# Token scores within halves of 64 rows: column halves of the array, a softmax over 64 columns, and mixing as two products with zero-padded weights

## The reference, cut to what matters

```python
xv = x.reshape(n, b, t, d).transpose(1, 0, 3, 2)        # t = 16, d = 192
q = jnp.einsum('bndt,st->bnds', xv, Wq) + bq            # s: 8
kv = jnp.einsum('bndt,st->bnds', xv, Wkv) + kv_bias     # k: 8, v: 8
q = q * scale
attn = jax.nn.softmax(jnp.einsum('bnds,bndr->bnsr', q, k), axis=-1)
out = q.transpose(0, 1, 3, 2) + jnp.einsum('bnsr,bndr->bnsd', attn, v)
```

## Time and profile before

| what | value |
|---|---|
| device time, median of 3 runs | 964.21 us (962.97 to 966.08) |
| the profiled execution: its own time | 967.46 us |
| its span, first to last instruction | 965.2 us, 25885 instructions |
| busy share: PE, PEld | 97%, 84% |
| busy share: DVE, ACT, POOL | 81%, 67%, 70% |
| mean granted TensorE clock | 0.988 |

### The profile page before, as it was taken

How to read it: one execution, slowest core, us unless ns; L and a number is a source line. 1 busy time by engine, 2 the same in 40 slices (tenths; PEclk the granted TensorE clock), 3 DMA queues, 4 the chain that set the end, 5 groups by cost and what they waited for, 6 DMA issues and landing times.

```text
span 965.2 us, 25885 instructions
## 1 busy us (share of the span) xinstructions
PE 934.8 (97%) x7402; PEld 814.2 (84%) x7402; DVE 781.2 (81%) x1996; ACT 645.7 (67%) x2501; POOL 673.6 (70%) x968
## 2 busy tenths in 40 slices
PE   5788999999999999999999999999999999999998
PEld 3667888889888889898888988888889888898877
DVE  3678888888888888888888888888888888888863
ACT  2456766676776676776667677667777666767763
POOL 2665777776677777677777767777767778776770
PEclk8899999999999999999999999999999999999999
DMA  6025444456444445544445554444554444555440
GB/s 199 24 70 143 129 121 126 127 149 160 134 130 120 129 128 160 156 121 126 129 121 149 160 138 131 117 128 129 159 158 121 130 125 123 145 160 146 110 118 17
DMA packets 193423, 124.68 MB, mean 129 GB/s; under 512 B 30720, under 2 KB 184960, under 8 KB 193408
## 3 DMA queue, kind: packets, MB, share of 16 engines
q1 hardware_dynamic: 190528, 121.05, 46.3%
q10 hardware_dynamic: 2880, 3.44, 1.1%
HBM read 69.39 MB, written 55.05 MB: 129 GB/s over the span
## 4 chain that ended last, share of the span: by engine, by line
PE 92%; DVE 3%; DMA 2%; issue 1%; POOL 1%; ACT 1%; SPq 1%; ACTq 0%; DVEq 0%; POOLq 0%
PE ring L1039 15%; PE bank L1058 13%; PE ring L1077 10%; PE bank L1251 7%; PE ring L1017 7%; PE ring L1251 7%; PE ring L1113 6%; PE ring L1157 4%; PE bank L1113 3%; PE ring L1163 3%; PE ring L1212 3%; PE ring L1182 3%; PE bank L1157 2%; PE bank L1233 2%; PE bank L1163 1%; PE bank L1203 1%
## 5 line engine op out<-in xcount | busy, mean ns | idle before, releaser
L335 ACT ACTIVATE E<-ring,m_neg 128x128 f32<-128x128 f32 x768 | 269.8, 383 | 9.9 <-DVE m_neg L684 8.9
L546 POOL TENSOR_TENSOR E<-E,e_rcp 128x512 f32<-128x512 f32 x158 | 175.6, 1111 | 91.5 <-DVE e_rcp L707 89.0
L538 POOL TENSOR_TENSOR qkT<-rot_c,rot_s 128x256 f32<-128x256 f32 x256 | 188.8, 738 | 20.1
L335 ACT ACTIVATION_READ_ACCUMULATOR E<-ring,m_neg 128x1 f32 x768 | 170.8, 222 | 0.0
L536 POOL TENSOR_TENSOR rot_s<-rot_s,rope_qs 128x256 f32<-128x256 f32 x192 | 140.8, 733 | 20.0 <-DVE rot_s L678 20.0
L1058 PE MATMUL bank<-wout_sb,G 128*128 128x192 f32 x744 | 152.0, 334 | 0.0
L684 DVE TENSOR_REDUCE m_neg<-ring 128x4 f32<-128x512 f32 x192 | 127.2, 676 | 11.2 <-PE ring L1077 11.2
L1058 PEld LDWEIGHTS bank<-wout_sb,G 128*128 128x128 f32 x744 | 118.7, 190 | 15.2 <-issue 11.5
L698 DVE STREAM_TRANSPOSE EB<-E 128x512 f32<-128x512 f32 x186 | 125.3, 689 | 1.5 <-POOL E L546 0.8
L1077 PE MATMUL ring<-qkT 64*128 64x128 f32 x1536 | 105.6, 285 | 0.4 <-POOL qkT L538 0.4
L1077 PEld LDWEIGHTS ring<-qkT 64*128 64x128 f32 x1536 | 93.2, 192 | 13.4 <-issue 9.1
(11 more groups left out here) (159 smaller groups left out, 2494.6 us busy)
## 6 DMA issues: line engine op xcount, KB each, us to landing
spill<-EB SPq DMA_DIRECT2D x186, 256.0 KB, 2.3
ET<-spill SPq DMA_DIRECT2D x248, 128.0 KB, 2.8
ET<-spill SPq DMA_DIRECT2D x248, 64.0 KB, 2.4
x_sb<-in_x_dram SPq DMA_DIRECT2D x64, 192.0 KB, 2.6
out_dram<-out_sb SPq DMA_DIRECT2D x31, 192.0 KB, 2.5
x_sb<-in_x_dram SPq DMA_DIRECT2D x64, 64.0 KB, 2.4
w_raw<-in_w_att_dram ACTq DMA_DIRECT2D x2, 608.0 KB, 5.8
win_raw<-in_w_in_dram ACTq DMA_DIRECT2D x2, 384.0 KB, 6.4
```

What stands on the lines that cost most here:

```text
L335: last = nc.scalar.activation(E[:, a, s * P:(s + 1) * P], RING[a][:, s * P:(s + 1) * P], ACT.Exp, bias=m_neg[:, a, s:s + 1], accum_out=e_s ...
L538: nc.gpsimd.tensor_tensor(qkT[:, b, :, a], rot_c[:, b, :, a], rot_s[:, b, :, a], ALU.add).then_inc(q_out, 1)
L546: nc.gpsimd.tensor_tensor(e, e, r, ALU.mult).then_inc(prob_out, 1)
```

## The change

Each query row only meets keys of its own half (rows 0 to 63 or 64 to 127), since blocks of 8 don't cross row 64. The changed kernel computes only the two 64x64 squares on the diagonal of each score matrix and keeps them beside each other: rows on 128 partitions, 64 columns per sequence. `tok_scores` issues eight calls of 64 output columns by 64 moving columns, with the lower and the upper column half of the array in turn, in place of four calls of 128 by 128. Mask, t_s, t_e, t_a, t_aT, t_c, t_d and bias_qv have 64 columns per sequence in place of 128. Because t_aT of both halves now shares its columns, `tok_mix` needs two products over 128 columns with weights bd_v[:, i] that are zero in the other half's rows, in place of one over 256. The layout of t_m turns from (a, i) to (i, a). At the start, bd_v takes two products of 64 partitions and two memsets on DVE.

```diff
-    blk = (row[:, None] // T2 == row[None, :] // T2)
+    blk = (row[:, None] % (P // 2) // T2 == row[None, 0:P // 2] // T2)
...
-        t_s, t_e, t_a, t_aT = (sb(n, [P, 2, P]) for n in ("t_s", "t_e", "t_a", "t_aT"))
+        t_s, t_e, t_a, t_aT = (sb(n, [P, 2, P // 2]) for n in ("t_s", "t_e", "t_a", "t_aT"))
...
-        t_c, t_d = sb("t_c", [P, 2, P]), sb("t_d", [P, 2, P])
+        t_c, t_d = sb("t_c", [P, 2, P // 2]), sb("t_d", [P, 2, P // 2])
...
-            nc.vector.tensor_tensor(bd_v[:].rearrange("p (b t) -> p b t", t=T), blk_keys[:].rearrange("p (b t) -> p b t", t=T),
-                                    wrep[:, 2 * T2:2 * T2 + T].rearrange("p (o t) -> p o t", o=1).broadcast_to([P, 8, T]),
-                                    ALU.mult).then_inc(s_bd, 1)
+            for i in range(2):
+                own = slice(i * (P // 2), (i + 1) * (P // 2))
+                nc.vector.tensor_tensor(bd_v[own, i].rearrange("p (b t) -> p b t", t=T),
+                                        blk_keys[own].rearrange("p (b t) -> p b t", t=T),
+                                        wrep[own, 2 * T2:2 * T2 + T].rearrange("p (o t) -> p o t", o=1).broadcast_to([P // 2, 8, T]),
+                                        ALU.mult).then_inc(s_bd, 1)
+                nc.vector.memset(bd_v[(1 - i) * (P // 2):(2 - i) * (P // 2), i], 0.0).then_inc(s_bd, 1)
...
-            nc.vector.transpose(t_aT[:].rearrange("p a (j c) -> p a j c", j=NB),
-                                t_a[:].rearrange("p a (j r) -> p a j r", j=NB)).then_inc(aT_out, 1)
+            nc.vector.transpose(t_aT[:].rearrange("p a (j c) -> p a j c", j=2),
+                                t_a[:].rearrange("p a (j r) -> p a j r", j=2)).then_inc(aT_out, 1)
...
                     for a in range(2):
-                        last = group(TOK_S[:, a * P:(a + 1) * P], (
-                            (qkT1[:, a, 0:P], qkT1[:, a, P:DP]), (qT2[:, a], kT2[:])))
+                        for k, (q, key) in enumerate(((qkT1[:, a, 0:P], qkT1[:, a, P:DP]), (qT2[:, a], kT2[:]))):
+                            for i in range(2):
+                                own = slice(i * (P // 2), (i + 1) * (P // 2))
+                                last = nc.tensor.matmul(TOK_S[own, a * (P // 2):(a + 1) * (P // 2)], q[:, own], key[:, own],
+                                                        start=(k == 0), stop=(k == 1))
                     last.then_inc(s_mm, 1)
...
-                    nc.tensor.matmul(TOK_M, bd_v[:], t_aT[:].rearrange("p a c -> p (a c)"),
-                                     start=True, stop=True).then_inc(m_mm, 1)
+                    for i in range(2):
+                        last = nc.tensor.matmul(TOK_M[:, i * P:(i + 1) * P], bd_v[:, i], t_aT[:].rearrange("p a c -> p (a c)"),
+                                                start=True, stop=True)
+                    last.then_inc(m_mm, 1)
```

More of the change, by code:

```diff
@@ L106, in program @@
         TOK_QK, TOK_REST = RING[1][:, 0:512], RING[1][:, 512:512 + DP]
[L107 removed]
+        TOK_S, TOK_M, TOK_H = RING[1][:, 512 + DP:512 + DP + P], B7[:, 0:DP], RING[0][:, 512:512 + 2 * D]
         HIDDEN = (RING[0][:, 1024:1536], B6[:], RING[1][:, 512:1024])
@@ L120, in program @@
         rope_kc, rope_ks, rope_qc, rope_qs = (sb(n, [P, P]) for n in ("rope_kc", "rope_ks", "rope_qc", "rope_qs"))
-        smask, blk = sb("smask", [P, P]), sb("blk", [P, P // 2])
+        smask, blk = sb("smask", [P, P // 2]), sb("blk", [P, P // 2])
         half_neg, warm = sb("half_neg", [P, 2]), sb("warm", [P, 2])
@@ L125, in program @@
         wrep, blk_keys = sb("wrep", [P, 2 * T2 + T]), sb("blk_keys", [P, P])
-        bd_qk, bd_v = sb("bd_qk", [P, P]), sb("bd_v", [P, P])
+        bd_qk, bd_v = sb("bd_qk", [P, P]), sb("bd_v", [P, 2, P])
         bqk_row, bias_rows = sb("bqk_row", [P, DP]), sb("bias_rows", [P, 1])
-        bias_sc, bias_qv, t_bias = sb("bias_sc", [P, 1]), sb("bias_qv", [P, P]), sb("t_bias", [P, 2])
+        bias_sc, bias_qv, t_bias = sb("bias_sc", [P, 1]), sb("bias_qv", [P, P // 2]), sb("t_bias", [P, 2])
         w_raw1, w_raw2 = sb("w_raw1", [P, NW]), sb("w_raw2", [P, NW])
@@ L552, in token_bias @@
                     need(pool, bias_sum, 2 * n)
-                    nc.gpsimd.tensor_tensor(t_c[:], t_a[:], bias_qv[:].rearrange("p (o c) -> p o c", o=1).broadcast_to([P, 2, P]),
+                    nc.gpsimd.tensor_tensor(t_c[:], t_a[:], bias_qv[:].rearrange("p (o c) -> p o c", o=1).broadcast_to([P, 2, P // 2]),
                                             ALU.mult).then_inc(bias_out, 1)
@@ L779, in tok_mixed @@
                     need(dve, h_mm, n)
-                    nc.vector.tensor_tensor(t_m[:].rearrange("p a i s -> p (a i) s"),
+                    nc.vector.tensor_tensor(t_m[:].rearrange("p i a s -> p (i a) s"),
                                             TOK_M.rearrange("p (x s) -> p x s", x=4),
@@ L801, in token_qk @@
                     if isinstance(p, int) and p == -1:
-                        dve.wait_ge(s_bd, 3)
+                        dve.wait_ge(s_bd, 6)
                     nc.vector.tensor_tensor(qkT1[:], TOK_QK.rearrange("p (a c) -> p a c", a=2),
@@ L1196, in tok_mix @@
                     if first == "tok":
-                        pe.wait_ge(s_bd, 3)
+                        pe.wait_ge(s_bd, 6)
                     if att and fin:
@@ L1211, in tok_h @@
                         for i in range(2):
-                            last = nc.tensor.matmul(TOK_H[i * (P // 2):(i + 1) * (P // 2), a * D:(a + 1) * D], t_m[:, a, i],
+                            last = nc.tensor.matmul(TOK_H[i * (P // 2):(i + 1) * (P // 2), a * D:(a + 1) * D], t_m[:, i, a],
                                                     x_sb[:, i, a], start=True, stop=True)
@@ L1374, in laid_out @@
         "bq_row": np.tile(tok_bq[None, :], (P, P // T2)),
-        "bv_row": np.tile(tok_bkv[None, :], (P, P // T2)),
+        "bv_row": np.tile(tok_bkv[None, :], (P, P // T2 // 2)),
         "w_att1": w_att[0:P], "w_att2": np.concatenate([w_att[P:D], w_att[P:D]], axis=0),
```

4 lines of the change are left out of this document (2 added, 2 removed).

## The result

The changed kernel takes 951.42 us (median of 6 runs, 950.03 to 952.64). The kernel before, run beside it, takes 964.38 (6 runs, 962.97 to 967.18). The ratio is 0.9843, with a 95% interval of 0.9827 to 0.9859. Against the 964.21 us of the prediction that is 949.1 us. The prediction said 953.9, from 950.5 to 960.5: right in the sign, too small in the size, and 1.4 us outside the range. The two medians alone stand 12.96 us apart, a ratio of 0.9866, just above that interval and inside the range (951.2 us); the record doesn't show where the difference between the two ratios comes from.

What follows compares the result with a forecast made beforehand. PE's own stream was taken to set the loop's time. Savings of 8.7 us (loop and pair 31), 0.3 (p = 1), 1.0 (p = 0) and 0.3 (p = -1) made 10.3: from median 964.21 to 953.9 us, range 950.5 to 960.5.

Steps and rivals of the forecast that it cites:

- a saving of 0.27 a step: tok_scores in each step: 0.885 us becomes 0.61, from a shape change, an exposed first load and 8 pairs at 0.058.
- (B): Rival: a pair stays at 0.111 us or the halves don't start together; about 967.5 us, slower; chance 0.09.
- (D): Rival: pairs near 0.09 us, so PE gains nothing and only some 2 us remain; 962.3 us; chance 0.06.
- The harsher form of (B): Rival: every pass costs at least 0.062 us, a pair 0.124; 971 us; chance 0.02 of the 0.09.
- a loss of 0.014: tok_mix in each step: two passes at 0.43 us become four at 0.444, 0.014 longer.
- a wait of 0.06 ... the wait goes: PE's wait for DVE's hn ahead of hn_turned: 0.06 us a step, gone because t_c loses half its columns.
- The x loads take a part: Loads of x ahead of tok_qk: late in some steps, so only 0.04 of the 0.06 at hn_turned is gained.
- (C): Rival: x loads, or v_tok and qkT at scores(0), take 0.15 of the 0.30 a step; 958.3 us; chance 0.13.
- Loop and pair 31: ... 8.7 us: The loop and pair 31: 29 steps, each saving 0.26 + 0.04 us, 8.7 us in all.
- In p = 0 ... 1.0 us in all: Step p = 0, token chain on the path: tok_scores, four DVE operations and two exponentials shorter, 1.0 us saved.
- In p = -1 ... 0.3: Step p = -1: the same small operations, partly under the weights' DMAs and warming matmuls, save 0.3 us.
- Step p = 1 has the same PE work: 0.3: Step p = 1: same PE work as a loop step, so the same saving of 0.3 us.

Runs made afterwards that it cites:

- the wide t_c alone: The changed kernel with POOL's t_c again computed over 256 columns, second half unused; 954.68 us, ratio 0.9869 to the kernel before.
- the third profile: The changed kernel run a third time with no edit; 950.19 us, ratio 0.9852 to the kernel before.
- its twin with the x loads first: The kernel before with the loads of x issued ahead of the second batch of transfers of attention probabilities; 964.66 us, ratio 0.9998.
- the first changed profile: The profiled execution of the changed kernel from its first measurement, with no further edit; median 951.42 us, ratio 0.9843.

## Why the prediction was right in sign and short in size

**`tok_scores`, "a saving of 0.27 a step": right.** 0.279, with the change of shape in front of it counted in. Each part holds: 0.095 for the change of shape (0.092), 0.055 for the first load, 0.058 a pair. A pair of 64 columns costs half of the shortest pair shown before, so the interpolation was the right choice between 0.053 and 0.111, and (B) and (D) are out. The harsher form of (B), by the rule of the Trainium skill in "TensorE: Matmul & The Clock Gate", section "Wait — 56ns, not 53.3ns?", is out as well: its 62 ns a MATMUL are for hardware decode off, and here 16 passes come at 0.029 us each, less than half of that.

**`tok_mix`, "a loss of 0.014": right,** 0.012.

**hn_turned, "a wait of 0.06 ... the wait goes": right,** and a little more: 0.070 ahead of it and 0.027 inside it, for the reason given (t_c beside hn), which the wide t_c alone undoes.

**The x loads take a part: right in kind, (C) in small.** The change alone is worth 0.369; the x loads take 0.087 of it in this profile (and 0.024 was lost there before), which leaves the 0.306. In the third profile they take 0.031. The forecast had 0.26 + 0.06 = 0.32, less 0.02. Two errors of some 0.05 cancel here, so the hit at 0.30 is partly luck.

**"Loop and pair 31: ... 8.7 us": right for the loop, short by 1 us at the end.** Steps p = 3 to 29 gave 8.3 and p = 2 took 0.1 more: 8.2. The part behind them gave 1.3, not 0.3. In the profile of before, PE stands 1.06 us before a transfer of attention probabilities (L1113) near 940.7 us, and no such gap is in the changed kernel. Nothing was tested there, but one run bears on it: the kernel before with its waits filled, all old shapes, has no such gap either, and its part behind p = 29 takes 76.94 us, like the changed kernel's 76.86, against 78.14 before. So that 1 us doesn't come from the narrow shapes as such; what decides it is open.

**The step that failed is the start: "In p = 0 ... 1.0 us in all. In p = -1 ... 0.3", and "Step p = 1 has the same PE work: 0.3".** The profile gave 5.0 where these make 1.6: 1.8 up to p = 0, 1.9 in it, 1.3 in p = 1. Two things were wrong. The chain was counted about right in p = 0 (0.8 against 1.0), but too small in p = 1 (1.1 against 0.3) and in p = -1 (0.6 against 0.3): in p = 1 PE waited 0.61 us for t_aT ahead of `tok_mix`, so the chain was on the path there, and the loop's 0.3 was the wrong price. And the sum left out the clock. The granted clock of the first slices is 0.8 in the earlier trace rows, and the sum has no term for it, as if the change left it alone. The clock moves with what PE does in its waits, as the filled ones show, and is worth about 3 us there in the old kernel. That in the changed kernel it is the shorter waits that raise it is argued from this, not shown: one of its three profiles has no better clock in p = 0 than the kernel before. The two profiles of before and the one of its twin with the x loads first arrive at p = 2 at 89.48 to 89.65; those of the changed kernel at 84.64, 87.28 and 81.96: 5.0 earlier on the average, spread over 5.3.

**The range was too narrow for the same reason.** It gave the first steps 0.5 to 3 us. They gave 2.3 to 7.6, and vary by more than the width of that range from one execution of the changed kernel to the next. The three ratios, 0.9843, 0.988 and 0.9852, are 949.1, 952.6 and 949.9 us of 964.21; one of them lies inside the range. Open stays what decides in a given execution where the 1.2 GHz stretches fall: the same program had p = 0 at 0.87, 0.93 and 1.00.

## What to carry to other kernels

Price a pass, a pair and a change of shape from differences of start times; with these, products in another shape were forecast here to 0.01 us, and halving the columns paid although the calls doubled and a change of shape was added. Then look for what is next late: a transfer that was worth next to nothing to move before the change was worth up to 2.5 us after it. Look also for waits in the single steps ahead of the loop: work that the loop hides was on the path there, in three steps and not in one. And where an engine waits in the first microseconds of a kernel, count the clock beside the chain: filling TensorE's waits with idle products gave 3.1 to 3.6 us in the old kernel, some 40% of what the change gave in the whole loop, and nothing measurable in the one whose chain was already shorter, where it moved DVE's t_a onto POOL's work.

## What was not expected of the hardware

- With two calls on one column half and then two on the other, sixteen passes cost 0.66 us, and 0.62 with the halves in strict turns. A call for the upper half starts beside one for the lower half that was issued two calls ahead of it.
- In the loop, t_a over half the columns takes longer. By the groups it took 705 ns for 256 columns before and is 804 for 128 (L829 in the groups of the changed kernel above), while t_s over the same columns, which reads PSUM, fell from 0.42 us to 292 ns (L818). t_a reads two operands in SBUF and now runs from 517.89 to 518.74, beside POOL's operations on the rotation, one of which runs from 517.87 to 518.59. In the filled p = 0 shown above it also ends 0.15 us behind POOL's operation (37.45 and 37.30). In p = 0 of the first changed profile it starts just as such an operation ends (37.40), and takes 0.29:

```profile
37.39 0.29 DVE L829 TENSOR_TENSOR t_a<-t_e,t_rs 128x128 f32<-128x128 f32 x1
```

So its length goes by where it falls beside POOL's work, and a chain moved by 0.14 us can cost 0.5 more. No run changes POOL's work beside t_a alone.
